# Two up-projections moved ahead of the output projection, and a biases' product moved behind the first down-projection

## The chip, the cores and the metric

The kernel runs on one core of one Trainium2 chip. The metric is the device time of one execution in microseconds (us), the median of several runs. The engines of the core are TensorE (PE, with its weight loads as PEld), VectorE (DVE), ScalarE (ACT), GpSimd (POOL) and SyncE (SP, which here only issues transfers).

## The reference

One transformer layer with modulation over x of 8 x 1024 x 256 (rows, tokens, channels), all in float32:

```
mod = silu(c) @ wmod                      # sa, ca, ga, sb, cb, gb per row; |ga|, |gb| >= 0.25
h = layernorm(x) * (1 + ca) + sa
x = x + ga * attention(h)
h = layernorm(x) * (1 + cb) + sb
x = x + gb * ffn(h)
```

The attention is linear: q and k of 16 heads (16 channels each) are scaled and clipped, Chebyshev polynomials are taken of both, of which the orders 1 to 5 have a weight, running sums over the tokens of T(k) v and of T(k) are built, and the output is the weighted sum of T(q) times the first, over the sum of T(q) times the second, followed by the output projection W_out.

The FFN has a shared expert and eight routed ones of 128 hidden channels: `silu(h W1 + b1) W2 + b2` for each. Every token takes its two best of the eight, weighted with sqrt(softplus(logit)):

```
hdn = silu(einsum('nd,edh->enh', h, rW1) + rb1)       # up-projection
y = einsum('enh,ehd->end', hdn, rW2) + rb2            # down-projection, second biases
routed = einsum('ne,end->nd', combine, y)
```

## The kernel before

The 8192 tokens are worked in 16 chunks of 512 (`CT`), two to a row, and number(i, p) = 2 i + p is a chunk's number. The program is a pipeline over chunks. `step(i, p, st)` exists once for each engine and does, for the stage of chunk c: the attention of chunk c; the first norm's transposes and the QKV projections of chunk c + 1 (`nxt`); the second norm, the router and its combine weights for chunk c - 1 (`prev`); and the nine experts of chunk c - 2 (`exp`). The dictionary `st` says which of these parts a stage has: two stages at the start (`FIRST`) and four at the end (`LAST`) have only some, twelve have all. The order of the work on each engine is the order in which its step is written out; there is no planner. Engines wait for each other with semaphores that count up.

Matrix products with float32 precision are split into high and low parts: `split_product` (line 1264) makes six matmuls of 512 columns of one product (two halves of the channels, and high x high, high x low, low x high). The high parts are written by ScalarE (`highs`, line 756), the low parts by VectorE from the same PSUM banks (`lows`, line 909): n1H, n1L for the first norm, n2H, n2L for the second. TensorE's queue in a full stage, in this order:

- up-projections of experts 0 and 1 (line 1264, inputs n2H, n2L, w1H, w1L) into the two banks of `ring`;
- `second_biases` (line 1372): four matmuls that put combine weights times second biases into the accumulators `acc`, with start set;
- transposes of the first norm (line 1255) into `tr`, behind the residual, which has read the projection from there; then up 2, down 0, four QKV projections, up 3, down 1;
- transposes of the second norm (line 1255), experts, router, head sums (line 1317), experts, the denominators (line 1330), experts 5 to 8;
- `project_out` (line 1341): eight products of the divided attention with W_out into `tr`, which wait for VectorE's `divide` (line 1029);
- `combine_by_expert` (lines 1353 and 1355): transposes of the split combine weights of chunk c - 1.

A down-projection (line 1383) of a routed expert waits until VectorE has multiplied the hidden state with the spread combine weights (`weigh_hidden`, line 1110). ScalarE writes that hidden state (`hidden`, silu, line 813) from the ring bank into one of three `hid` slots. The ring banks are used in a fixed order of 15 uses per full stage (`RING`, `ring_of`), and each use waits until the one two before has been copied out.

VectorE's queue at the turn of a stage: `divide` (1029), `output` (line 1119, the experts' sum times the gate), the odd orders of the next keys (925, 927); then, in the next stage, `residual` (1037, projection plus x, in two halves), statistics (367), odd orders of the queries, a weighting (943), `lows` of the first norm (909), more weightings and running sums (962), `weigh_hidden` of experts 1 and 2, a running sum, `lows` of the second norm.

The combine weights go to all partitions by way of DRAM: ScalarE copies them out of PSUM (`combine_rows`, 828 and 829), SyncE writes them to `cf_rows` (588), waits, and spreads them into `cfw` (592, for experts 1 to 6) and later the last two (598). GpSimd adds the experts' output to the stored x by an accumulating DMA (706). The inverse denominators go through DRAM in the same way (576, 581).

Of the kernel before, what the change touches and what calls it, by code (L numbers as in the profile page):

```python
# [8 lines left out]
P = 128  # L9
# [76 lines left out]
def build(nc, x_d, w_in_d, w_out_d, rout_d, ebias_d, sw1_d, sb1_d, sw2_d, sb2_d,  # L86
# [8 lines left out]
    with ctx:  # L95
# [185 lines left out]
        def number(i, p):  # L281
            return CB * i + p
# [463 lines left out]
        def _(act):  # L746
# [83 lines left out]

            def step(i, p, st):
                use = ring_of(i, p, st)
                nxt, prev, exp = later(i, p, 1), later(i, p, -1), later(i, p, -2)
# [9 lines left out]

                silu(0)
                silu(1)
                if qkv:
# [28 lines left out]
                if p == 1 and (not isinstance(i, int) or i < B):  # L875
                    row_biases(i, use if ffn else None)
                if second:
                    combine_rows(*prev)
# [5 lines left out]
            for q in range(2):  # L884
                for which in range(3):
                    square(0, 0, q, which)
            for i, p, st in FIRST:
                if number(i, p) == 1:
                    act.wait_ge(late_biases, 2)
                step(i, p, st)  # L890
            with act.Fori(1, B - 1) as i:
                for p in range(CB):
                    step(i, p, ALL)
            for i, p, st in LAST:
                step(i, p, st)

# [344 lines left out]
        def _(pe):  # L1241
# [123 lines left out]
            def second_biases(i, p):  # L1365


                c = number(i, p)
                pe.wait_ge(cf_ready, 2 * c + 2)
                ge(pe, ffn_gated, 2 * c)  # L1370
                for t in range(NT):
                    mm(acc[t // 2][:, t % 2], cfR[:, t * P:(t + 1) * P], r2[:, :], start=(t % 2 == 0), stop=False,
                       skip_group_check=True)

            def expert_down(i, p, use, e):

                c = number(i, p)
                if e:
                    pe.wait_ge(hidw_ready, E * c + e)
                else:  # L1380
                    pe.wait_ge(ring_copied, use["e0"][0] + 1)
                for t in range(NT):
                    last = mm(acc[t // 2][:, t % 2], hid[:, e % NG, t * P:(t + 1) * P], w2[:, e], start=False,  # L1383
                              stop=(e == E), skip_group_check=True)
                last.then_inc(expert_done, 1)

            def step(i, p, st):
                use = ring_of(i, p, st)
                nxt, prev, exp = later(i, p, 1), later(i, p, -1), later(i, p, -2)
# [7 lines left out]

                if ffn:
                    expert_up(*exp, use, 0)
                    expert_up(*exp, use, 1)  # L1400
                    second_biases(*exp)
                if qkv:
                    transposes(0, *nxt)
                if isinstance(i, int) and number(i, p) == 0:
                    bias_products()
                expert(0)
                if qkv:
                    for half in HALVES[:4]:
                        project(*nxt, use, half)
# [21 lines left out]
                expert(7)  # L1431
                expert(8)
                if attn_:
                    project_out(i, p)
# [13 lines left out]
            for half in HALVES:  # L1448
                project(0, 0, CHUNK0, half)
            for i, p, st in FIRST:  # L1450
                step(i, p, st)
            pe.wait_ge(late_weights, 2)
            pe.wait_ge(in_w2, 32)
            pe.wait_ge(s_r2, 4)
            for p in range(CB):
                step(1, p, ALL)
            with pe.Fori(2, B - 1) as i:
                for p in range(CB):
                    step(i, p, ALL)
            for i, p, st in LAST:  # L1460
                step(i, p, st)

# [24 lines left out]
```

## Time and profile before

| | us |
|---|---|
| median of 3 runs | 990.74 (985.78 to 991.19) |
| profiled execution | 988.04 |
| its span, first to last instruction | 986.3 |
| PE busy | 863.2 (88%) |
| DVE busy | 832.3 (84%) |
| POOL busy | 461.1 (47%) |
| ACT busy | 440.8 (45%) |
| mean granted TensorE clock | 0.955 |

All times of single instructions come from the profiled execution. Busy times are those of instructions that compute; matmuls are pipelined and their ends are modelled, so the modelled end of a group can lie after the start of the next. An idle time is given in brackets with what ended it.

### The profile page before, as it was taken

To read this page: it belongs to the slowest core of one execution; us is meant where nothing else is said; L and a number is where in the kernel's file an instruction comes from. 1 tells how busy PE (TensorE), PEld (TensorE's weight loads), DVE (VectorE), ACT (ScalarE), POOL (GpSimd) and SP (SyncE) were. 2 spreads that over 40 slices of the span, in tenths; PEclk is the share of its full clock that TensorE was granted. 3 is DMA by queue.
4 is the path that set the end of the run, shared out by engine and by line. 5 is a ranking of instruction groups with operands and counts; after the bars stand their busy time and mean duration, and the time that the engine had idled before them with its cause. 6 is when DMAs were issued, how large, how long until landed. Compare 5 with 4: busy or idle time off the path is not lost. (4 is left out here: it accounts for less than half of the span.)

```text
span 986.3 us, 14280 instructions
## 1 busy us (share of the span) xinstructions
PE 863.2 (88%) x4377; PEld 641.4 (65%) x4377; DVE 832.3 (84%) x1319; ACT 440.8 (45%) x637; POOL 461.1 (47%) x631
## 2 busy tenths in 40 slices
PE   3862658999898999999999999899999999978995
PEld 3641426676666767676767676686767676747784
DVE  2478798999899999999999999999999999987421
ACT  4253425363545545353635455554535363431420
POOL 2013445273546547472747365554837175453210
PEclk9777778999999999999999999999999999999998
DMA  7104133344452546353543536353634243443431
GB/s 256 49 1 87 43 68 127 75 102 128 74 160 66 151 88 161 65 142 77 117 120 72 149 69 176 68 150 80 167 65 125 69 103 113 79 128 75 126 108 21
DMA packets 51948, 101.03 MB, mean 102 GB/s; under 512 B 5347, under 2 KB 34606, under 8 KB 49846
## 3 DMA queue, kind: packets, MB, share of 16 engines
q1 hardware_dynamic: 35106, 65.45, 20.4%
q0 software_dynamic: 15360, 33.56, 19.9%
q10 hardware_dynamic: 1428, 1.43, 0.5%
q8 instruction: 18, 0.29, 0.1%
q14 instruction: 36, 0.29, 0.1%
HBM read 57.68 MB, written 17.58 MB: 76 GB/s over the span
## 5 line engine op out<-in xcount | busy, mean ns | idle before, releaser
L1383 PE MATMUL acc<-w,hid 128*128 128x256 f32 x1152 | 272.6, 382 | 14.6 <-DVE hid L1110 14.6
L1383 PEld LDWEIGHTS acc<-w,hid 128*128 128x128 f32 x1152 | 215.1, 190 | 58.9 <-DVE hid L1110 27.0
L813 ACT ACTIVATE hid<-ring,b1row 128x512 f32<-128x512 f32 x144 | 98.5, 684 | 180.3 <-PE ring L1264 179.0
L657 POOL DMA_DIRECT2D feat<-feat x48 | 46.5, 968 | 273.8 <-DVE feat L987 132.3
L1110 DVE TENSOR_TENSOR hid<-hid,cfw 128x512 f32<-128x512 f32 x128 | 92.9, 728 | 43.6 <-DMA cfw<-cf_rows 28.1
L768 ACT ACTIVATE feat<-ring,bqkv 128x512 f32<-128x512 f32 x96 | 66.1, 689 | 116.6 <-PE ring L1264 116.6
L1341 PE MATMUL tr<-wo_g,feat 128*128 128x256 f32 x256 | 67.1, 421 | 47.1 <-DVE feat L1029 47.1
L1264 PE MATMUL ring<-n2H,w1H 128*128 128x512 f32 x288 | 102.5, 437 | 0.0
L962 DVE TENSOR_TENSOR_SCAN feat<-zero,carry,feat 128x512 f32<-128x512 f32 x80 | 99.2, 1289 | 0.0
L962 DVE TENSOR_TENSOR_SCAN feat<-zero,feat 128x512 f32<-128x512 f32 x80 | 94.5, 1230 | 0.0
L1341 PEld LDWEIGHTS tr<-wo_g,feat 128*128 128x128 f32 x256 | 52.7, 211 | 61.0 <-DVE feat L1029 45.0
L1264 PE MATMUL ring<-n2H,w1L 128*128 128x512 f32 x288 | 90.5, 395 | 0.0
L1264 PE MATMUL ring<-n2L,w1H 128*128 128x512 f32 x288 | 90.4, 395 | 0.0
L1317 PE MATMUL tr<-feat,const 128*32 128x512 f32 x640 | 90.0, 608 | 0.0
L1264 PE MATMUL ring<-n1H,winH 128*128 128x512 f32 x192 | 68.4, 438 | 16.2 <-issue 14.5
L338 POOL TENSOR_TENSOR ms<-stats 128x4 f32<-128x4 f32 x32 | 42.3, 1323 | 73.3 <-DVE stats L367 68.6
L788 ACT ACTIVATE feat<-feat,const 128x1024 f32<-128x1024 f32 x64 | 70.0, 1141 | 1.0
L645 POOL TENSOR_TENSOR feat<-feat 128x1024 f32<-128x1024 f32 x16 | 53.3, 3330 | 30.1 <-DVE feat L927 30.1
L1264 PE MATMUL ring<-n1L,winH 128*128 128x512 f32 x192 | 62.7, 408 | 0.0
L1264 PEld LDWEIGHTS ring<-n2L,w1H 128*128 128x128 f32 x288 | 54.4, 189 | 12.5
L1264 PE MATMUL ring<-n1H,winL 128*128 128x512 f32 x192 | 62.5, 407 | 0.0
L1264 PEld LDWEIGHTS ring<-n2H,w1L 128*128 128x128 f32 x288 | 54.2, 188 | 12.6
(152 smaller groups left out, 1550.8 us busy)
## 6 DMA issues: line engine op xcount, KB each, us to landing
feat<-feat POOLq DMA_DIRECT2D x48, 512.0 KB, 4.6
cfw<-cf_rows SPq DMA_DIRECT2D x16, 1280.0 KB, 7.7
xin<-in_L_attn_x SPq DMA_DIRECT2D x16, 512.0 KB, 9.5
feat<-inv_rows SPq DMA_DIRECT2D x32, 256.0 KB
out<-x SPq DMA_DIRECT2D x16, 512.0 KB, 8.6
cfw<-cf_rows SPq DMA_DIRECT2D x16, 512.0 KB, 3.6
out<-fin POOLq DMA_DIRECT2D x16, 512.0 KB, 6.1
cfw<-cf_rows SPq DMA_DIRECT2D x16, 256.0 KB, 4.7
```

What stands on the lines that cost most here:

```text
L338: nc.gpsimd.tensor_tensor(t(0), m0, m1, ALU.add).then_inc(mv_steps[n], 1)
L645: g.tensor_tensor(f(W + 4), f(KT5), f(V0), ALU.mult).then_inc(weighted5, 1)
L657: g.dma_start(f(into), f(of), accum_op=ALU.add).then_inc(added[n], 16)
L768: a.activation(feat[:, (K0 + p, Q0 + p, V0)[m // 2], m % 2], ring[bank][:, :], ACT.Identity, bias=col(bqkv[:, (2, 3, 0, 1, 4, 5)[m]], i)). ...
L788: a.activation(f((qa, qb)[which - 1]), f(s), ACT.Square, bias=cv["biases"][:, which - 1:which]).then_inc(squares, 1)
L813: a.activation(hid[:, e % NG], ring[bank][:, :], ACT.Silu, bias=b1row[:, e:e + 1]).then_inc(ring_copied, 1)
L962: last = v.tensor_tensor_scan(feat[:, W + n, h], zero[:, 0:1].to_broadcast([P, CT]), feat[:, W + n, h], carry[:, n, h:h + 1] if p else 0.0 ...
L1110: v.tensor_tensor(hid[:, e % NG], hid[:, e % NG], cfw[:, (e - 1) % NW], ALU.mult).then_inc(hidw_ready, 1)
L1264: last = mm(out, w, x, start=(n == 0), stop=(n == len(terms) - 1))
L1317: last = mm(tr[q][g_ * QS:(g_ + 1) * QS, :], cv["headsum"][:, (r // HPH) * QS:(r // HPH + 1) * QS], feat[:, srcs[n], h], start=(n < 4 and ...
L1341: last = mm(tr[t // 2][:, (t % 2) * D:(t % 2 + 1) * D], attn[:, k, t * P:(t + 1) * P], wo_g[:, k], start=(k == 0), stop=(k == KD - 1))
L1383: last = mm(acc[t // 2][:, t % 2], hid[:, e % NG, t * P:(t + 1) * P], w2[:, e], start=False, stop=(e == E), skip_group_check=True)
```

## The change

On TensorE, the up-projections of experts 0 and 1 of a stage are issued in the stage before it: behind the last down-projection (`expert(8)`) and ahead of `project_out`, or, in a stage without attention, ahead of `combine_by_expert`. For that `step` is also given the next stage's parts (`st_next`) and its uses of the ring (`use_next`). `second_biases` moves from the head of the stage to behind the first down-projection. That down-projection now starts the accumulation (`start=True` for the first half of each bank) and takes over the wait for the accumulators to be free (`ffn_gated`); the biases' product continues it. On ScalarE, silu 0 and 1 of a stage move likewise to the end of the stage before, behind `row_biases` and ahead of `combine_rows`. Two waits for weights at the start are placed anew. VectorE, GpSimd and SyncE keep their programs.

```diff
             # ScalarE
-            def step(i, p, st):
-                use = ring_of(i, p, st)
+            def step(i, p, st, st_next):
+                use, use_next = ring_of(i, p, st), ring_of(*later(i, p, 1), st_next)
...
-                silu(0)
-                silu(1)
                 if qkv:
                     highs(0, *nxt)
                 silu(2)
...
                 if p == 1 and (not isinstance(i, int) or i < B):
                     row_biases(i, use if ffn else None)
+                if st_next["ffn"]:
+                    hidden(*prev, use_next, 0)
+                    hidden(*prev, use_next, 1)
                 if second:
                     combine_rows(*prev)
             # TensorE
                 pe.wait_ge(cf_ready, 2 * c + 2)
-                ge(pe, ffn_gated, 2 * c)
                 for t in range(NT):
-                    mm(acc[t // 2][:, t % 2], cfR[:, t * P:(t + 1) * P], r2[:, :], start=(t % 2 == 0), stop=False,
+                    mm(acc[t // 2][:, t % 2], cfR[:, t * P:(t + 1) * P], r2[:, :], start=False, stop=False,
                        skip_group_check=True)
...
                     pe.wait_ge(ring_copied, use["e0"][0] + 1)
+                    ge(pe, ffn_gated, 2 * c)
                 for t in range(NT):
-                    last = mm(acc[t // 2][:, t % 2], hid[:, e % NG, t * P:(t + 1) * P], w2[:, e], start=False,
-                              stop=(e == E), skip_group_check=True)
+                    last = mm(acc[t // 2][:, t % 2], hid[:, e % NG, t * P:(t + 1) * P], w2[:, e],
+                              start=(e == 0 and t % 2 == 0), stop=(e == E), skip_group_check=True)
...
-                if ffn:
-                    expert_up(*exp, use, 0)
-                    expert_up(*exp, use, 1)
-                    second_biases(*exp)
                 if qkv:
                     transposes(0, *nxt)
                 if isinstance(i, int) and number(i, p) == 0:
                     bias_products()
                 expert(0)
+                if ffn:
+                    second_biases(*exp)
...
                 expert(8)
+                if st_next["ffn"]:
+                    if isinstance(i, int) and number(i, p) == 1:
+                        pe.wait_ge(late_weights, 2)
+                    expert_up(*prev, use_next, 0)
+                    expert_up(*prev, use_next, 1)
                 if attn_:
                     project_out(i, p)
```

## Rows read from the trace of the kernel before

**Rows 1.** The page: busy us, share of the span, instructions of an engine.
```profile
PE 863.2 (88%) x4377; PEld 641.4 (65%) x4377; DVE 832.3 (84%) x1319; ACT 440.8 (45%) x637; POOL 461.1 (47%) x631
```
**Rows 2.** Waits, whole span: who waited for whom, us in total, times, longest.
```profile
PE tr L1341 <- DVE feat L1029: 47.1, 16, 13.3
...
DVE n2L L909 <- ACT n2H L756: 15.0, 14, 3.4
```
**Rows 3.** Timeline of PE: output projections and one QKV product; start, us, [idle before].
```profile
152.68 5.78 PE L1341 MATMUL tr<-wo_g,feat 128*128 128x256 f32 x16 [13.26 <-DVE feat L1029]
...
166.14 0.80 PE L1264 MATMUL ring<-n1H,winH 128*128 128x512 f32 x2
...
208.25 3.72 PE L1341 MATMUL tr<-wo_g,feat 128*128 128x256 f32 x16 [0.95 <-DVE feat L1029]
...
262.18 5.41 PE L1341 MATMUL tr<-wo_g,feat 128*128 128x256 f32 x16 [1.95 <-DVE feat L1029]
...
853.43 3.72 PE L1341 MATMUL tr<-wo_g,feat 128*128 128x256 f32 x16 [1.99 <-DVE feat L1029]
...
906.59 5.41 PE L1341 MATMUL tr<-wo_g,feat 128*128 128x256 f32 x16 [3.11 <-DVE feat L1029]
```
**Rows 4.** Timeline of PE over the turn of one inner stage.
```profile
532.48 3.72 PE L1341 MATMUL tr<-wo_g,feat 128*128 128x256 f32 x16 [1.13 <-DVE feat L1029]
...
536.39 0.71 PE L1264 MATMUL ring<-n2H,w1H 128*128 128x512 f32 x2
...
539.35 0.74 PE L1372 MATMUL acc<-r,cfR 50*128 50x256 f32 x4
...
542.34 1.89 PE L1383 MATMUL acc<-w,hid 128*128 128x256 f32 x8
543.88 0.81 PE L1264 MATMUL ring<-n1H,winH 128*128 128x512 f32 x2
```
**Rows 5.** Timeline of DVE over the same turn.
```profile
528.62 0.69 DVE L1110 TENSOR_TENSOR hid<-hid,cfw 128x512 f32<-128x512 f32 x1
...
535.89 1.27 DVE L1037 TENSOR_TENSOR x<-tr,xin 128x512 f32<-128x512 f32 x2
...
541.80 1.40 DVE L909 SCALAR_TENSOR_TENSOR n1L<-tr,mods,n1H 128x512 fp32r<-128x512 f32 x2
...
550.09 1.15 DVE L1110 TENSOR_TENSOR hid<-hid,cfw 128x512 f32<-128x512 f32 x1 [1.66 <-DMA cfw<-cf_rows]
...
554.36 1.41 DVE L909 SCALAR_TENSOR_TENSOR n2L<-tr,mods,n2H 128x512 fp32r<-128x512 f32 x2 [0.76 <-ACT n2H L756]
```
**Rows 6.** Timeline of DVE behind the projection at 152.68.
```profile
158.50 0.69 DVE L1037 TENSOR_TENSOR x<-tr,xin 128x512 f32<-128x512 f32 x1 [1.31 <-PE tr L1341]
...
163.83 1.40 DVE L909 SCALAR_TENSOR_TENSOR n1L<-tr,mods,n1H 128x512 fp32r<-128x512 f32 x2
```
**Rows 7.** Timeline of POOL: issues of the output's accumulating DMA, inner stage and last.
```profile
535.74 1.35 POOL L706 DMA_DIRECT2D out<-fin  x1 [0.85 <-POOL split L690]
...
946.70 1.33 POOL L706 DMA_DIRECT2D out<-fin  x1 [2.90 <-DVE fin L1119]
```
**Rows 8.** Timeline of SP: issues of the combine weights' copy and of their spread.
```profile
537.37 0.29 SPq L588 DMA_DIRECT2D cf_rows<-cfT  x1
541.83 0.82 SPq L592 DMA_DIRECT2D cfw<-cf_rows  x2
```
**Rows 9.** The chain that ended last, 906 to 980: start, us, what.
```profile
945.85 1.43 DMA cf_rows<-cfT
...
947.71 8.66 DMA cfw<-cf_rows
```
**Rows 10.** Windows: stretch, us, busy of each engine, then PEclk, the granted clock.
```profile
260.00:266.00 6.00, 4.05 (x12) 3.11 (x11) 5.06 (x7) 0.99 (x2) 3.60 (x7) 0.73 0.02 1
851.00:857.00 6.00, 4.01 (x20) 3.15 (x19) 5.03 (x7) 1.04 (x1) 3.54 (x7) 1.00 0.01 3
```

More of the change, by code:

```diff
@@ L886, in _ @@
                     square(0, 0, q, which)
-            for i, p, st in FIRST:
+            for n, (i, p, st) in enumerate(FIRST):
                 if number(i, p) == 1:
                     act.wait_ge(late_biases, 2)
-                step(i, p, st)
+                step(i, p, st, FIRST[1][2] if n == 0 else ALL)
             with act.Fori(1, B - 1) as i:
                 for p in range(CB):
-                    step(i, p, ALL)
-            for i, p, st in LAST:
-                step(i, p, st)
+                    step(i, p, ALL, ALL)
+            for n, (i, p, st) in enumerate(LAST):
+                step(i, p, st, LAST[n + 1][2] if n + 1 < len(LAST) else some())
         @block.vector
@@ L1381, in expert_down, with step @@
                     pe.wait_ge(ring_copied, use["e0"][0] + 1)
+                    ge(pe, ffn_gated, 2 * c)
                 for t in range(NT):
-                    last = mm(acc[t // 2][:, t % 2], hid[:, e % NG, t * P:(t + 1) * P], w2[:, e], start=False,
-                              stop=(e == E), skip_group_check=True)
+                    last = mm(acc[t // 2][:, t % 2], hid[:, e % NG, t * P:(t + 1) * P], w2[:, e],
+                              start=(e == 0 and t % 2 == 0), stop=(e == E), skip_group_check=True)
                 last.then_inc(expert_done, 1)
-            def step(i, p, st):
-                use = ring_of(i, p, st)
+            def step(i, p, st, st_next):
+                use, use_next = ring_of(i, p, st), ring_of(*later(i, p, 1), st_next)
                 nxt, prev, exp = later(i, p, 1), later(i, p, -1), later(i, p, -2)
@@ L1449, in _, with stages @@
                 project(0, 0, CHUNK0, half)
-            for i, p, st in FIRST:
-                step(i, p, st)
-            pe.wait_ge(late_weights, 2)
+            def stages(steps, after):
+                for n, (i, p, st) in enumerate(steps):
+                    step(i, p, st, steps[n + 1][2] if n + 1 < len(steps) else after)
+            stages(FIRST, ALL)
+            pe.wait_ge(s_r2, 4)
             pe.wait_ge(in_w2, 32)
-            pe.wait_ge(s_r2, 4)
-            for p in range(CB):
-                step(1, p, ALL)
+            stages([(1, p, ALL) for p in range(CB)], ALL)
             with pe.Fori(2, B - 1) as i:
[L1458 to L1461, printed above, removed]
+                stages([(i, p, ALL) for p in range(CB)], ALL)
+            stages(LAST, some())
 _INS = ['L0_attn_x', 'L0_attn_W_in', 'L0_attn_W_out', 'L0_ffn_routing_W', 'L0_ffn_expert_bias', 'L0_ffn_sW1',
```

## Prediction, made before the changed kernel ran

> **What bounds the kernel now.** I read the page's busy shares first: TensorE 88%, VectorE 84% [rows 1]. Both are averages with start and end in them, so I went on to the waits. TensorE's one regular wait is the one the change aims at: it stands before the output projection until VectorE has divided (L1029), 47.1 us over 16 times [rows 2]. Four of the sixteen are special (13.02, 13.26, 1.95, 3.11; three of them in rows 3); the other twelve, 0.95 to 1.99, leave 15.8 us, 1.31 each. VectorE's regular wait is for the second norm's high parts, 15.0 us in 14 times [rows 2].
>
> Then I laid the timelines of both engines over one inner stage. A stage is 53.8 us, (853.43 - 208.25) / 12 [rows 3]. TensorE goes from the projection at 532.48 to the first QKV matmul at 543.88 without a gap [rows 4]. VectorE, too, has no gap from the division to the low parts that end at 543.20; its only waits are 1.66 before the second expert's weighting (a DMA) and 0.76 before the second low parts at 554.36 [rows 5], and from there it is busy until the next division. So a stage is a loop through both: division, projection on TensorE, QKV, second norm, second low parts, then VectorE alone. The reader should see that VectorE has nearly as little slack as TensorE: the QKV product could start 0.68 earlier (543.88 less 543.20), and no more, before it waited for VectorE.
>
> **The projection is moved back.** The two up-projections with what follows take 539.35 - 536.39 = 2.96 us [rows 4]. The gap before the projection is 1.13 by the profile, but a group's modelled end lies after the moment the next can start: 542.34 + 1.89 - 543.88 = 0.35 [rows 4]. So the up-projections find 1.13 + 0.35 = 1.48 us of room, and the projection starts 2.96 - 1.48 = 1.48 later, at 533.96. The last down-projection can't move forward to make room: its hidden state is weighted at 528.62 + 0.69 [rows 5].
>
> **What waits for it.** VectorE's residual takes the two halves of the projection. Where it waited for the second half, it started 158.50 - 152.68 = 5.82 after the projection's start, for a group of 5.78 [rows 3, 6]; for one of 3.72 that is 3.76. So the second half is there at 537.72. VectorE wanted it at 535.89 + 1.27 - 0.68 = 536.48 (0.68 is one of the two) [rows 5]: a new stall of 1.24 us, with all of VectorE's queue behind it: statistics, odd orders, a weighting, and the low parts, which now end at 544.44. TensorE is by then through its queue: transposes wait for the residual (about 538.4), and transposes, third up-projection, first down-projection and the moved biases' product take 543.88 - 539.35 = 4.53 together [rows 4]; it is at the QKV product at about 543.0 and waits there for 544.44. The product starts 0.56 later than before (544.44 less 543.88), with about 0.1 of handover 0.66.
>
> From there to the second low parts it is TensorE and ScalarE back to back (554.36 - 543.88 = 10.48), so these come 0.66 later; VectorE's own arrival (553.60, plus the stall of 1.24 less what the wait of 1.66 takes up) is earlier. Behind them VectorE has no wait up to the next division but, in some stages, the one for the spread inverse, which moves along with VectorE. The mean gap is 1.31 instead of 1.13, so a mean stage loses 0.66 - 0.18 = 0.48.
>
> **The combine weights are late too.** Their transposes follow the projection, so the copy to DRAM (537.37) is issued up to 1.48 later. If the spread weights land as much later, VectorE reaches the second low parts at 553.60 + 1.48 = 555.08, a loss of 0.72 in this stage. If they land as before, 0.66 stands. What decides is the output's accumulating DMA, issued at 535.74 by GpSimd, which doesn't move [rows 7]: the small copy (16 KB) takes 4.46 us to the next issue behind it [rows 8], against 1.43 at the end, where it goes ahead of it [rows 9]. A copy issued later has less of it to wait for, so I take most of this as hidden. The Trainium skill says the same as a rule (DMA: Bandwidth & Descriptors, "Issuing engines are not separate DMA queues"): transfers of all engines share 16 DMA engines and interleave. By the rule the copy's landing hardly moves; were the queues separate, it would move by the full 1.48. The trace bears the rule out by 4.46 against 1.43.
>
> Twelve ordinary stages: 0.46 to 0.69 each, 5.5 to 8.3; I take 0.5, **+6.0**.
>
> **Free edits.** The second biases' product only changes places with work between the same two waits. Silu 0 and 1 move ahead of the combine rows on ScalarE; their inputs are there at 533.96, its next input only after the projection at 537.9, so that costs nothing where a projection lies between. Without that cover it would be one silu's tail, about 0.3, at the end below.
>
> **The end.** The last boundary has no output projection and no gap: the up-projections go before the combine transposes, and the chain runs through these, the copy, the spread (8.66 us) and so to the end [rows 9]. So +2.96 +0.3. Besides, the copy was issued 0.85 ahead of the output's DMA (945.85 against 946.70 [rows 7, 9]) and would now be behind it, where it took 4.46: between 0 and 3.0 more, part of it given back since the spread then meets less traffic. Bounds 2.9 to 6; I take **+4**.
>
> **The three special boundaries.** At 152.68 the gap takes the up-projections whole; the QKV product at 166.14 then starts behind the low parts' end at 165.23 [rows 3, 6]: **-0.8**. At 262.18 and 906.59 the projection took 5.41 instead of 3.72 [rows 3], under a granted clock of 0.73 over the six us, so partly at the half rate (1.2 GHz); another stage with the same gap kept 1.00 [rows 10]. If the filled gap keeps the clock up, each gives back up to 1.7, if not nothing (at 262.18 the projection would start 0.66 later, 2.96 - 1.95 - 0.35, and at 906.59 on time): **-0.5** and **-1.2**.
>
> Sum: 6.0 + 4 - 0.8 - 0.5 - 1.2 = +7.5 us. The profiled execution took 988.04 (span 986.3), so it would be 995.5; the median of the runs is 990.74, 2.7 above, which gives **998 us**. The forecast's own range is +4.6 (5.5 + 2.9 less 0.8 and 1.5 twice) to +13.5 (8.3 + 6 less 0.8).
>
> **Rivals.**
> 1. *The gain is real* (faster). If VectorE's low parts weren't the limit, the QKV product would start 1.48 earlier in each stage; twelve of 1.66 (room 1.31 + 0.35) and both clock falls, 23.3 us, less 4 at the end: -19, 971. It would take a slack on VectorE of more than 2 us where rows 4 and 5 show 0.68; it decides only if the residual doesn't wait for the moved projection. 0.10.
> 2. *Absorbed.* The stall stays under 0.7 us (half a projection handed over earlier than 3.76, or up-projections quicker next to others), the QKV product doesn't move, and only the end and the start count: 4 - 2.5 = +1.5, 992. For it: the first half is already there in time, and slack and loss are within 1 us of each other. Against it: the wait at 158.50, which ended with the projection's last half and not before [rows 6]. 0.19.
> 3. *Everything late.* The weights land 1.48 later each time and the end costs 6: 8.3 + 6 - 0.8 = +13, 1004. Against it: rows 7 to 9. 0.12.
> 4. *The clock falls in the new gap.* TensorE now waits 0.5 at the transposes and 1.4 before the QKV product. A gap of 1.95 was once followed by a fall worth 1.69 [rows 3, 10]. If that happens in nine of the twelve stages, 9 x 1.69 = 15 come on top of +7.5: +22, 1013. Against it: the twelve gaps of 0.95 to 1.99 behind which the group took its 3.72, and the new ones are shorter. 0.06. The Trainium skill (TensorE: Matmul & The Clock Gate, "Why this matters for your kernels") asks for no idle gaps between bursts of matmuls to keep the clock. By it the change gains where it closes the gaps of 1.95 and 3.11 (the -1.7 each) and risks the fall of rival 4 where it opens two. The trace agrees only in part: 1.95 fell, 1.99 didn't.
>
> **Chances.** Forecast 0.53, rivals 0.10, 0.19, 0.12, 0.06. A difference of 0.5%, about 5 us, is what a measurement of this kernel tells from none. Faster by more: rival 1, 0.10. Within: rival 2 and the forecast's lowest part, 0.23. Slower: the rest, 0.67. The range from 988 to 1007 leaves out rivals 1 and 4 and little else; it reaches down to rival 2 and up past rival 3.
>
> **What would show it.** In the changed profile: TensorE's wait before the projection is nearly gone, and a wait for n1L (L909) of 1 to 1.5 stands before the QKV product in most stages; VectorE waits for the projection (L1037) about 1.1 in each stage; the wait for n2H at L909 shrinks only slightly or vanishes; projection start to QKV start falls from 11.4 to about 10.6, while projection to projection grows from 53.8 by half a us; copy to spread at L588/L592 takes 3 to 3.5 us instead of 4.5. It is wrong if VectorE doesn't wait at L1037, if stages don't grow, or if TensorE's clock differs in the middle of the run.

## The result: 13 us slower, in the direction forecast and nearly twice its size

The changed kernel takes 1003.06 us in the median of 4 runs (1002.09 to 1003.26), beside 989.84 for the kernel before in the same set: ratio 1.0132, 95% interval 1.0093 to 1.017. Its profiled execution took 1002.91 (span 1001.2), 14.9 more than the one before. The forecast was +7.5, with a range up to 1007.

Page of the changed kernel, busy shares. Most line numbers of VectorE and TensorE are higher by one in the kernel after (projection L1342, division L1030, residual L1038, low parts L910, up-projections L1265, down-projections L1384):

```profile
PE 867.9 (87%) x4377; PEld 643.1 (64%) x4377; DVE 846.2 (85%) x1319; ACT 440.1 (44%) x637; POOL 444.4 (44%) x631
```

The shares are those of [rows 1] within a point, but for GpSimd's (44% instead of 47%), and don't show where 14.9 us went. The waits say more (engine, line, releaser: us in total, times, longest):

```profile
DVE hid L1111 <- DMA cfw<-cf_rows: 25.7, 7, 11.6
DVE x L1038 <- PE tr L1342: 18.8, 18, 1.6
...
DVE n2L L910 <- ACT n2H L756: 7.7, 12, 3.4
```

The wait that was aimed at [rows 2] is gone but for the first two stages (12.56 and 8.71) and 0.26 at the last, and VectorE now waits for the projection 18.8 us in 18 pieces. The same turn of an inner stage as in [rows 4], PE of the changed kernel:

```profile
535.89 3.62 PE L1342 MATMUL tr<-wo_g,feat 128*128 128x256 f32 x16
...
540.41 1.09 PE L1256 MATMUL tr<-const,ntok 128*128 128x128 f32 x8 [0.46 <-DVE x L1038]
...
542.74 1.89 PE L1384 MATMUL acc<-w,hid 128*128 128x256 f32 x8
544.55 0.73 PE L1372 MATMUL acc<-r,cfR 50*128 50x256 f32 x4
546.62 0.73 PE L1265 MATMUL ring<-n1H,winH 128*128 128x512 f32 x2 [1.33 <-DVE n1L L910]
```

And DVE, as in [rows 5]:

```profile
533.07 1.34 DVE L1030 TENSOR_TENSOR feat<-feat 128x512 f32<-128x512 f32 x2 [0.27 <-DMA feat<-inv_rows]
...
538.07 0.69 DVE L1038 TENSOR_TENSOR x<-tr,xin 128x512 f32<-128x512 f32 x1 [0.19 <-issue]
539.66 0.69 DVE L1038 TENSOR_TENSOR x<-tr,xin 128x512 f32<-128x512 f32 x1 [0.90 <-PE tr L1342]
...
544.98 1.40 DVE L910 SCALAR_TENSOR_TENSOR n1L<-tr,mods,n1H 128x512 fp32r<-128x512 f32 x2
...
557.01 1.41 DVE L910 SCALAR_TENSOR_TENSOR n2L<-tr,mods,n2H 128x512 fp32r<-128x512 f32 x2 [0.30 <-ACT n2H L756]
```

The projection starts 2.82 behind the division (before 1.4 to 1.5) and without a gap; the residual's second half waits 0.90, the transposes 0.46, the QKV product 1.33 for the low parts. Projection to QKV product is 546.62 - 535.89 = 10.73 (before 11.40), and the second low parts come 23.94 behind the division (before about 23.4).

### The profile page after: what moved, and what is told of

Same layout as the page of the kernel before. It is cut to its first block and busy times, and to the rows that moved or that the text cites. A ratio compares the mean times of both kernels' runs of the same rounds, so it can differ in the third digit from the quotient of the medians.

```text
span 1001.2 us, 14280 instructions
## 1 busy us (share of the span) xinstructions
PE 867.9 (87%) x4377; PEld 643.1 (64%) x4377; DVE 846.2 (85%) x1319; ACT 440.1 (44%) x637; POOL 444.4 (44%) x631
## 3 DMA queue, kind: packets, MB, share of 16 engines
q10 hardware_dynamic: 1428, 1.43, 0.5%
## 5 line engine op out<-in xcount | busy, mean ns | idle before, releaser
L1384 PE MATMUL acc<-w,hid 128*128 128x256 f32 x1152 | 277.9, 386 | 29.7 <-DVE hid L1111 29.7
L1384 PEld LDWEIGHTS acc<-w,hid 128*128 128x128 f32 x1152 | 217.2, 192 | 76.5 <-DVE hid L1111 43.5
L1111 DVE TENSOR_TENSOR hid<-hid,cfw 128x512 f32<-128x512 f32 x128 | 88.8, 695 | 43.7 <-DMA cfw<-cf_rows 25.7
L963 DVE TENSOR_TENSOR_SCAN feat<-zero,carry,feat 128x512 f32<-128x512 f32 x80 | 107.7, 1396 | 0.0
L1265 PE MATMUL ring<-n2H,w1H 128*128 128x512 f32 x288 | 104.3, 443 | 0.0
L1265 PE MATMUL ring<-n1H,winH 128*128 128x512 f32 x192 | 67.2, 432 | 32.9 <-issue 17.8
L963 DVE TENSOR_TENSOR_SCAN feat<-zero,feat 128x512 f32<-128x512 f32 x80 | 92.3, 1201 | 0.0
L1265 PE MATMUL ring<-n2L,w1H 128*128 128x512 f32 x288 | 91.2, 398 | 0.0
L1265 PE MATMUL ring<-n2H,w1L 128*128 128x512 f32 x288 | 90.9, 397 | 0.0
L1342 PE MATMUL tr<-wo_g,feat 128*128 128x256 f32 x256 | 62.6, 401 | 21.5 <-DVE feat L1030 21.5
L338 POOL TENSOR_TENSOR ms<-stats 128x4 f32<-128x4 f32 x32 | 33.3, 1039 | 88.1 <-DVE stats L367 83.5
L1342 PEld LDWEIGHTS tr<-wo_g,feat 128*128 128x128 f32 x256 | 51.4, 202 | 31.0 <-DVE feat L1030 22.9
L645 POOL TENSOR_TENSOR feat<-feat 128x1024 f32<-128x1024 f32 x16 | 53.0, 3315 | 30.0 <-DVE feat L928 30.0
L1265 PEld LDWEIGHTS ring<-n1H,winH 128*128 128x128 f32 x192 | 36.7, 199 | 44.8 <-issue 35.7
L1265 PEld LDWEIGHTS ring<-n2H,w1L 128*128 128x128 f32 x288 | 54.8, 190 | 12.9
L1265 PEld LDWEIGHTS ring<-n2L,w1H 128*128 128x128 f32 x288 | 54.8, 190 | 12.7
L1265 PEld LDWEIGHTS ring<-n2H,w1H 128*128 128x128 f32 x288 | 50.0, 191 | 19.4 <-issue 11.7
```

The lines of the kernel that those rows point to most:

```text
L338: nc.gpsimd.tensor_tensor(t(0), m0, m1, ALU.add).then_inc(mv_steps[n], 1)
L645: g.tensor_tensor(f(W + 4), f(KT5), f(V0), ALU.mult).then_inc(weighted5, 1)
L963: last = v.tensor_tensor_scan(feat[:, W + n, h], zero[:, 0:1].to_broadcast([P, CT]), feat[:, W + n, h], carry[:, n, h:h + 1] if p else 0.0 ...
L1111: v.tensor_tensor(hid[:, e % NG], hid[:, e % NG], cfw[:, (e - 1) % NW], ALU.mult).then_inc(hidw_ready, 1)
L1265: last = mm(out, w, x, start=(n == 0), stop=(n == len(terms) - 1))
L1342: last = mm(tr[t // 2][:, (t % 2) * D:(t % 2 + 1) * D], attn[:, k, t * P:(t + 1) * P], wo_g[:, k], start=(k == 0), stop=(k == KD - 1))
```

## Where the 14.9 us are

I took the start of each division as the mark of a stage (numbered 0 to 15 here) and compared the two profiled executions.

| stretch | before | after | difference |
|---|---|---|---|
| start to division 0 | 96.62 | 95.63 | -1.0 |
| 0 to 2 | 110.23 | 110.52 | +0.3 |
| 2 to 3 | 53.94 | 53.60 | -0.3 |
| 3 to 4 | 55.96 | 55.12 | -0.8 |
| 4 to 14, ten stages | 535.22 | 544.94 | +9.7 |
| 14 to 15 | 53.27 | 52.36 | -0.9 |
| 15 to the end of the span | 81.06 | 89.03 | +8.0 |

The ten stages split once more, at the second low parts: +5.1 from division to these (0.51 a stage in the mean, 0.1 to 0.8 in each), +4.65 from these to the next division. The latter lies in the odd stages. Four of the five took 29.7 to 30.2 there and now take 31.2 to 31.5; the fifth, stage 9, had taken 31.3 before and takes 31.1. The even stages are 0.1 shorter in the mean.

One execution of each kernel is little for such small differences. The kernel with the biases alone and the one with only the last boundary changed (both below) leave the ups of these ten stages where they were: 539.6 and 536.3 beside the 535.2 of before, mean 537.0. The up-projections alone and the last boundary as before leave them moved: 546.5 and 544.0 beside 544.9, mean 545.1. So the ten stages lose about 8, and the two parts are +3.2 (0.32 a stage) and +4.8 in the mean of three executions each.

One of the odd stages in the kernel before, first the timeline of DVE, then that of POOL:

```profile
501.00 1.41 DVE L909 SCALAR_TENSOR_TENSOR n2L<-tr,mods,n2H 128x512 fp32r<-128x512 f32 x2 [0.72 <-ACT n2H L756]
502.33 1.21 DVE L987 SCALAR_TENSOR_TENSOR feat<-feat 128x1024 f32<-128x1024 f32 x1
503.46 1.22 DVE L983 TENSOR_TENSOR feat<-feat 128x1024 f32<-128x1024 f32 x1
```
```profile
500.71 1.30 POOL L713 TENSOR_TENSOR wo_g<-wo,gates 128x512 f32<-128x512 f32 x1 [0.45 <-DMA gates<-gate_rows]
```

The same stage of the changed kernel:

```profile
495.06 3.43 DVE L946 SCALAR_TENSOR_TENSOR feat<-feat 128x1024 f32<-128x1024 f32 x1
498.41 0.68 DVE L1111 TENSOR_TENSOR hid<-hid,cfw 128x512 f32<-128x512 f32 x1
...
503.13 1.22 DVE L988 SCALAR_TENSOR_TENSOR feat<-feat 128x1024 f32<-128x1024 f32 x1
504.26 2.32 DVE L984 TENSOR_TENSOR feat<-feat 128x1024 f32<-128x1024 f32 x1
```
```profile
494.50 2.90 POOL L645 TENSOR_TENSOR feat<-feat 128x1024 f32<-128x1024 f32 x1
503.15 2.35 POOL L713 TENSOR_TENSOR wo_g<-wo,gates 128x512 f32<-128x512 f32 x1 [5.75 <-DMA gates<-gate_rows]
```

Once per row of the batch, in the odd stages, GpSimd scales W_out by the gates (L713). Before, that took 1.30 us and began about where VectorE waits for the second high parts (22.9 to 23.9 behind the division in four rows of six), so that it ran beside the low parts, which took their 1.41 all the same; in the changed kernel it comes at 25.2 to 26.0 in all six. Here it starts at 503.15, under VectorE's order products, and each holds up the other: L713 takes 2.35, and L984, begun at 504.26, ends 1.08 behind it at 506.58 and takes 2.32 instead of 1.22. In stage 9 the product before it (L988) is the stretched one (2.27), in stage 13 the weighting of a hidden state behind it (L1111, 1.78); in stage 9 of the kernel before it was L987 (2.32). L713 comes later here because VectorE, late by the stall, now starts its weighting L946 (495.06) just behind GpSimd's L645 (494.50): 3.43 instead of 1.22. The weighting of the next hidden state is late by that, and SP's load of the gates waits in its queue behind the weights' issue that this releases. SP of before, then of after:

```profile
495.88 0.33 SPq L598 DMA_DIRECT2D cfw<-cf_rows  x1
496.25 0.91 SPq L569 DMA_DIRECT2D gates<-gate_rows  x2
```
```profile
499.11 0.33 SPq L598 DMA_DIRECT2D cfw<-cf_rows  x1
499.49 0.91 SPq L569 DMA_DIRECT2D gates<-gate_rows  x2
```

The Trainium skill has the rule (SBUF — State Buffer, "Who interferes with whom"): a VectorE instruction with two SBUF inputs and a GpSimd instruction that reads SBUF shut each other out for a whole instruction, and the one begun first wins. These rows agree: L984 ends 1.08 behind L713, and L946 1.09 behind L645's end at 497.40.

All traces together bear it out. In the eleven traces of kernels that scale all of W_out (the experiments below among them) there are 55 such odd stages, five in each. In 27 of them L713 starts 24.4 or more behind the division, and from the second low parts to the next division they take 31.0 to 32.0. In the other 28 it starts at 23.9 or before, and they take 29.2 to 30.5. The changed kernel has five of the first kind in five, the kernel before one in five.

The end, in the chain of the changed kernel (start, us, what), against [rows 9]:

```profile
926.93 3.15 PE acc L1384 x8
930.08 1.40 PE tr L1256 x8
...
957.02 3.83 DMA cf_rows<-cfT
960.92 4.81 DMA cfw<-cf_rows
966.57 3.78 PE acc L1384 x8
970.36 2.20 PE ring L1265 x6
972.55 1.73 PE acc L1384 x8
```

The copy of the combine weights (957.02) takes 3.83 now, and the output's DMA was issued 2.2 ahead of it (954.81; for before [rows 7, 9]). Two groups on the chain, at 926.93 and 966.57, take 3.15 and 3.78 where the group takes 1.7 to 2.0 else. TensorE had stood idle before both, and the windows show its clock (the stretch, its length, busy of PE, PEld, DVE, ACT and POOL, PEclk, DMA share, GB/s):

```profile
926.90:930.90 4.00, 3.97 (x13) 3.28 (x14) 0.69 (x1) 0.00 (x0) 0.00 (x0) 0.59 0.67 251
966.50:970.50 4.00, 3.93 (x9) 3.20 (x10) 1.31 (x3) 0.00 (x0) 0.00 (x0) 0.50 0.16 69
```
```profile
926.93 3.15 PE L1384 MATMUL acc<-w,hid 128*128 128x256 f32 x8 [3.90 <-DVE hid L1111]
...
966.57 3.78 PE L1384 MATMUL acc<-w,hid 128*128 128x256 f32 x8 [5.12 <-DVE hid L1111]
```

A granted clock of 0.50 is the lower level, 1.2 GHz; at the same places of the kernel before it was 1.00.

From division 15 to the third down-projection of the last stage (972.39 after, 957.21 before) is 60.22 against 51.97, +8.25:

- the up-projections and a silu ahead of the last combine transposes: 2.76 + 0.28 = +3.0
- the boundary before it: +1.2 by the time of the copy's issue (D + 44.85 against D + 40.61, less the 3.0)
- the copy behind the output's DMA +2.4, but TensorE now waits for the first of the two transfers of the spread, not the second, -4.2: together -1.8
- from those weights to the third down-projection of the stage 6.61 instead of 0.79, +5.8: one more expert stands behind them (3.2), and half clock stretches it (3.78 + 2.20 on the chain instead of 1.99 + 1.40, 2.6).

Another 0.28 comes back behind that.

## Experiments

Each was timed in five rounds beside the kernel before, which took 989.26, 990.49 and 987.70 in the median in the three sets. Diffs are against the changed kernel, but for the first and for the smaller scaling on the kernel before.

**The biases alone** (on the kernel before).

```
 stage head:
-                    second_biases(*exp)          # behind expert_up(..., 1)
...
                 expert(0)
+                if ffn:
+                    second_biases(*exp)
...                                               # start= of the group moves to down-projection 0
```

> Only the second biases' product is moved behind the first down-projection; both up-projections stay at the head of the stage. My theory (the loss comes from the projection issued late behind the up-projections) expects no change: TensorE's queue from the projection to the QKV product is as long as before (11.4 us), 988 to 991. A theory in which the down-projection that now starts the accumulation, or the wait for the accumulators moved with it, costs something expects part of the 13 us here.

990.26 us, ratio 1.0005 (0.9977 to 1.0032): no cost by itself that this can tell. Its profiled execution spent 53.96 in each of the ten stages, 0.44 more than the one of the kernel before, with medians 1 apart. So much do two executions of like kernels differ; two of its five odd stages have the late scaling.

**The up-projections alone.** The same edit undone on the changed kernel; ups and silus stay ahead.

> Only the up-projections and their silus are moved ahead; the second biases' product stays at the head of the stage and starts the accumulation. My theory expects the whole loss here: 1002 to 1004, with the same stall of about 0.9 us before the second half of the residual and a QKV product that waits for n1L. The wait of 0.46 us at the first norm's transposes should be filled by the biases' product in part. If the loss needs both edits, the time is nearer to 990.

999.95 us, ratio 1.0114 (1.0083 to 1.0145): most of the loss, though 2 below the expected range. Its profiled execution was the slowest of the five. Its ten inner stages take 54.64 each, as the changed kernel's 54.49. Its end took 84.8 from division 15, and shows what the changed kernel's 89.0 is made of. Chain of this kernel:

```profile
931.38 1.99 PE acc L1384 x8
...
959.79 3.95 DMA cf_rows<-cfT
963.80 4.47 DMA cfw<-cf_rows
...
969.11 1.99 PE acc L1384 x8
971.11 1.39 PE ring L1265 x6
```

The copy is as slow (3.95), the order is the same, and TensorE waited before 969.11 too (3.23), but the clock held. So the end costs 84.84 - 81.06 = +3.8 without the two falls, and the falls carry most of the other 4.

**One up-projection ahead.**

```
                     hidden(*prev, use_next, 0)
-                    hidden(*prev, use_next, 1)
...
                     expert_up(*prev, use_next, 0)
-                    expert_up(*prev, use_next, 1)
...                                               # both back to their places of before
```

> The changed kernel, but only up-projection 0 (and silu 0) is issued ahead; up-projection 1 stays at the head of the next stage. One takes 1.48 us, about what there is of room before the projection (1.31 + 0.35). My theory: the projection is on time, VectorE doesn't stall at the residual, and the QKV product can start up to 0.6 earlier than before the change, bounded by n1L: 0.3 to 0.6 in each of 11 stages gained, 1.2 to 3 lost at the end: 984 to 990. If the loss were proportional to what is moved (by any cause that counts instructions and not room) it would be half of 13: 996.

988.49 us, ratio 0.9992 (0.9965 to 1.0019). The residual doesn't wait; the QKV product starts 12.28 behind the division instead of 12.9 and waits 0.65 for the low parts: of the room of 0.68 read from rows 4 it won 0.6, and the low parts hold it there. A stage keeps 0.24 of that: the ten take 53.28 each (before 53.52).

**The last boundary as before.**

```
-                if st_next["ffn"]:
+                if st_next["ffn"] and not (isinstance(i, int) and i == B):
...                                               # ups 0, 1 and silus 0, 1 of that stage at its head
```

> The changed kernel, but at the last boundary (stage 16 to 17, without an output projection) both up-projections and their silus stay at the head of the last stage, as before the change. From the trace of the changed kernel the part from the last division to the end is 89.0 us against 81.1 before. My theory: 2.8 of it is the up-projections in front of the combine transposes, 2.4 the copy of the weights that now falls behind the output's accumulating DMA, 2.7 a TensorE that has waited 5.1 us and restarts at the half rate, 1.2 the same at the boundary before. So the tail is back to about 82.3 and the time is 995.5 to 997.5. If the end is late for what happened earlier, nothing changes: 1003.

996.55 us, ratio 1.0067 (1.0041 to 1.0093). The stretch behind division 15 is 82.2 instead of 89.0. It still has the clock fall at the boundary before the last (group of 3.55 behind a wait of 3.96, at 927.76). SP and POOL of this kernel: the copy goes first again and takes 1.49 to the next issue:

```profile
954.65 0.28 SPq L588 DMA_DIRECT2D cf_rows<-cfT  x1
956.14 0.79 SPq L592 DMA_DIRECT2D cfw<-cf_rows  x2
```
```profile
955.50 1.33 POOL L706 DMA_DIRECT2D out<-fin  x1 [2.89 <-DVE fin L1123]
```

**The up-projections behind the projection**, ahead of the combine transposes.

```
+                if attn_:
+                    project_out(i, p)
                 if st_next["ffn"]:
...
-                if attn_:
-                    project_out(i, p)
```

> The changed kernel, but with both up-projections between the output projection and the combine transposes: the projection is on time, the combine weights are 2.96 us late (more than the 1.2 of the changed kernel). Theory of the late projection: no stall at the residual, the QKV product starts 11.4 after the projection as before; what is left is the end (about +7) and some wait for the late weights, 995 to 1001. Theory of the late combine weights: the loss per stage is larger than in the changed kernel, 1010 or more.

1001.75 us, ratio 1.0145 (1.0109 to 1.018), 0.75 outside the first range. VectorE of this kernel:

```profile
537.87 1.34 DVE L1030 TENSOR_TENSOR feat<-feat 128x512 f32<-128x512 f32 x2
...
542.75 1.28 DVE L1038 TENSOR_TENSOR x<-tr,xin 128x512 f32<-128x512 f32 x2
...
548.67 1.40 DVE L910 SCALAR_TENSOR_TENSOR n1L<-tr,mods,n1H 128x512 fp32r<-128x512 f32 x2
```

The residual has both halves at once, the QKV product starts 12.99 behind the division, and the second low parts 23.1 to 23.5: the loss ahead of these is gone. The weights came only a little later: their copy starts 9.3 behind the division (6.3 before), their spread at 10.7 to 11.5 (9.3 to 11.0 before). The rest, +0.41 per stage, is the stretched L984 (2.32) in all five odd stages. But L946 isn't stretched in this kernel. VectorE of stage 7 (division at 483.44):

```profile
499.69 1.22 DVE L946 SCALAR_TENSOR_TENSOR feat<-feat 128x1024 f32<-128x1024 f32 x1
...
502.23 1.94 DVE L1111 TENSOR_TENSOR hid<-hid,cfw 128x512 f32<-128x512 f32 x1 [1.32 <-DMA cfw<-cf_rows]
```

Here the weighting of the hidden state is late because it waits for the spread weights and then takes 1.94; SP issues the gates at 504.57, 21.1 behind the division, and the scaling starts at 25.0. So the stretched L946 is one way to a late scaling, and late weights are another; what they share is the late weighting that SP waits for.

The total is no better than the changed kernel's, since this execution had two early clock falls (projections of 5.41 in stages 2 and 3; +5.2 by division 4) and an end of 89.7.

**A smaller scaling of W_out, on the changed kernel and on the kernel before.** From the second row on GpSimd scales one column of W_out only, so the rest of the projection's weights keep the first row's gates; left out is all but one column of that product.

```
+                if isinstance(i, int) and i == 0:
                     g.tensor_tensor(wo_g[:, :, :], wo[:, :, :], ga, ALU.mult).then_inc(wo_ready, 1)
+                else:
+                    g.tensor_tensor(wo_g[:, :, 0:1], wo[:, :, 0:1], gates[:, 0:1, 0:1]...
```

> The changed kernel, with GpSimd's scaling of W_out by the row's gate cut to one column for all rows but the first (left out: the scaling of the other 255 columns; the output of rows 1 to 7 is projected with the first row's gate). In the changed kernel's trace this instruction (1.3 to 2.4 us) falls beside a product of VectorE (2.3 instead of 1.2 us) in six stages of seven. If the two engines shut each other out there, six times 1.1 us go: 996 to 998. If VectorE's product is slow for another reason (its own operands, a DMA), the time stays at 1003.

> The kernel before, with the same cut of the W_out scaling (the output of rows 1 to 7 is projected with the first row's gate). There the scaling fell into VectorE's own wait before the second low parts in four stages of six and beside a product in two or three. If that is why the change lost more than the late projection explains, the cut gives only 2 to 3 us here, 986 to 988, less than half of what it gives on the changed kernel.

On the kernel before 987.59, ratio 0.9973 (0.9945 to 1.0), 2.9 less than the kernel before in its set. On the changed one 1001.17, ratio 1.0108 (1.0072 to 1.0144), which is 2 us less than the change and not 6, and the intervals overlap. The time on the kernel before is the expected one, but the cut gave no more on the changed kernel than there, against both expectations. The stage times say something else. The stretched L984 is gone from all stages, and the odd ones take 29.7 to 30.3 behind the second low parts (31.1 to 31.5 in the changed kernel), also where the small scaling starts as late as 25.9. But four stages (4, 7, 9, 12) lost the gain ahead of them. TensorE of this kernel in one, and the window:

```profile
323.64 0.73 PE L1375 MATMUL acc<-r,cfR 50*128 50x256 f32 x4
325.71 0.72 PE L1268 MATMUL ring<-n1H,winH 128*128 128x512 f32 x2 [1.34 <-DVE n1L L913]
326.28 1.01 PE L1268 MATMUL ring<-n1L,winH 128*128 128x512 f32 x2
327.09 1.05 PE L1268 MATMUL ring<-n1H,winL 128*128 128x512 f32 x2
```
```profile
326.00:330.00 4.00, 4.00 (x12) 3.09 (x12) 4.00 (x5) 0.69 (x1) 3.92 (x4) 0.57 0.93 337
```

Behind the new gap of 1.34 before the QKV product the clock fell, and the second low parts came at 25.3 to 25.6 instead of 24.0 (24.5 in stage 7, whose projection had come early). The window's clock was 0.57 or 0.58 in all four. In the changed kernel the same gap stands in nearly every inner stage, and the clock kept 1.00 in the three windows taken (from 328, 382 and 437). The ten stages took 545.0 in this execution, as the changed kernel's 544.9: what the smaller scaling gave, the clock took. So the stretched product is what the scaling does to the stage; the total doesn't prove its price.

**One up-projection ahead, at all boundaries but the last**, the edits of the third and fourth together.

> One up-projection (and silu 0) issued ahead at all boundaries but the last, the biases' product behind the first down-projection. The same with the last boundary included took 988.5; its stages are 0.24 us shorter than before the change and its end is 1.1 longer. I expect the 1.1 to 2 us of the end back: 986.5 to 987.5, 2 to 3 us below the kernel before, about what five rounds can just tell. A theory in which any work moved ahead of the projection costs expects 989 or more.

982.61 us, ratio 0.9917 (0.9887 to 0.9947), faster than the kernel before by 0.8%, more than expected. It was run again beside the one-up kernel, since their first profiles had nearly the same end (82.6 and 82.2) and so didn't seem to say what set them apart.

> One up-projection ahead at all boundaries but the last, again. If the version really beats both kernels: 0.990 to 0.995 of before. If its first result was helped by scatter: 0.996 to 0.999, and the same as the kernel with one ahead everywhere.

> The same kernel as in the run with one up-projection ahead at every boundary, beside the kernel with one ahead at all but the last. In the profiles both had the same last stretch (82.2 and 82.6 us), so what set them apart in the medians (988.5 against 982.6) is not placed. If the last boundary costs what it seems to, this one is again 0.5 to 0.8% slower than the other, 0.999 of the kernel before; if the difference was scatter between the two sets of runs, the two come out within 0.3% of each other, both at 0.994 to 0.997 of before.

Again 982.88, ratio 0.9946 (0.9916 to 0.9976), against 986.34, ratio 0.9976 (0.995 to 1.0001), for one up everywhere. Both sets have it faster than before. Against the one-up kernel it is 0.35% faster, between the two expectations, and the intervals overlap. Its first profile is 5.8 below the one before: 3.7 between divisions 0 and 4 (the fall at 262 is avoided), 1.7 in the ten stages (53.35), 1.75 ahead of division 0, which is scatter, and -1.6 behind division 15. The one-up kernel's second profile had an end of 85.6: its group at 916.03 took 3.78 where the first run's at 914.77 took 1.99. The same instructions meet the fall in one execution and not in another.

What the last boundary costs with one up can be read once the falls are set apart. The end of 82.2 (one up everywhere) had none, the end of 82.6 (all but the last) had one at the boundary before:

```profile
912.67 3.68 PE L1386 MATMUL acc<-w,hid 128*128 128x256 f32 x8 [2.54 <-DVE hid L1113]
```

From this group to the next down-projection on the chain it is 5.94, against 4.26 without a fall, so the fall cost 1.7. Without it the last copy would have gone out about 40.2 behind division 15 instead of 41.84; with one up at the last boundary it went out at 41.55. That is 1.4, the time of one up-projection, and from the copy to the end of the span both take 40.6 to 40.8. The rest of the 3.5 between the medians is not placed.

**Only the last boundary** changed (the rest as in the kernel before, with the biases moved).

```
-                if st_next["ffn"]:
+                if st_next["ffn"] and isinstance(i, int) and i == B:
...                                               # all other stages begin as before
```

> Kernel before with the second biases behind the first down-projection, and the two up-projections and silus ahead only at the very last boundary, where no output projection lies between. If the end term of the changed kernel is the last boundary's own (its combine transposes 2.8 later, the small copy behind the output's DMA, one more expert behind the weights, and TensorE's slower clock behind the wait), this costs 6 to 7 us against the kernel before: ratio 1.006 to 1.007, and from the last division to the end of the span 87 to 88 us instead of 81. If it costs only the 2.8 to 3 of the up-projections themselves, 1.003 and 84. If the end term needs the other boundaries as well, 1.000 and 81 to 82.

993.36 us, ratio 1.0059 (1.0029 to 1.0088), and 86.3 from division 15 to the end: +5.3. The copy again takes 3.81, the wait before the second down-projection 4.64, and that group 3.19. It misses its range by a little. The kernel that put this boundary back had gained 6.8 by its end; 0.9 of the 1.5 between the two is the fall, which cost 2.6 there and 1.7 here (959.26 to 964.30, against 3.38 without one).

## Why the prediction was right, and what it mis-sized

The direction and the first link were right. The size was not: of the 14.9 us between the profiles the sum had 7.5. The time fell within the range because the range had been drawn past the third rival, whose number (1004) is nearly the measured one, while its mechanism, weights that land 1.48 later each time, did not happen. That part is luck.

**The late projection: right.** Forecast: second half 3.76 behind the projection's start (measured 3.77), QKV product held by the low parts, 0.66 later (0.68 in the stage shown), 0.5 a stage. Measured 0.51 in this pair of executions and 0.32 in the mean of three executions each, so the agreement to the hundredth is chance. With the residual unstalled (ups behind the projection) the loss vanished; with half the work ahead it turned into a small gain.

**The combine weights: right in outcome, not in the reason.** The copy went out about 1.2 later, and its spread followed after 2.4 (540.68 to 543.07) instead of 4.46 [rows 8] or the 3 to 3.5 forecast, so the spread came earlier than before and the weighting didn't wait. The forecast held GpSimd's issue still; in this stage it went out 3.37 behind the division instead of 4.73. The Trainium skill's rule cited in the forecast fits the end as well: the copy took 3.83 where it was issued 2.2 behind the output's DMA and 1.43 where it went ahead. It doesn't say when the copy lands; the last section has that from the traces.

**A term put at nothing: +4.65 in ten stages.** I followed VectorE's stall to the low parts and wrote that behind them VectorE has no wait, so that the stage loses the delay and no more. I did not ask what GpSimd does while VectorE is late. Its scaling of W_out had run in and beside a wait of VectorE's, and now starts under its products. That a late scaling costs the stage 1.2 us in the mean (31.3 against 30.05 behind the second low parts) is shown by the 55 stages, and that it goes with the scaling by the kernels with the small one. How the scaling comes to be late is read from the traces: the weighting that releases SP's queue is late, here by the stretched L946, with the ups behind the projection by late weights. No run moved the scaling by itself.

**The end: the mis-sized term.** Forecast +4 and, for a clock fall not had at 906.59, -1.2: +2.8. Measured +8.0. The +4 was good: the last boundary alone cost 5.3 with a fall of 1.7 in it. The -1.2 failed. The kernel with the last boundary as before has that term by itself, and its end costs +1.1, a fall included; in the up-projections' run, without a fall, the last copy's issue (43.43 less the 3.0 of the ups, against 40.61) gained 0.2. The projection did take 3.72 instead of 5.41, and the copy of the combine weights was issued 1.69 earlier behind the division. But it was now 3.05 behind the output's DMA instead of 4.74, and took 3.38 to the next issue instead of 1.84. The weights were there only 0.5 earlier (14.02 behind the division, before 14.52). With two up-projections fewer ahead of them, TensorE stood 3.90 and met a fall there; another followed at 966.57. This is the forecast's fourth rival at a place where it hadn't been expected; in its own place, before the QKV product, it did not appear in the three windows of the changed kernel, but did in four stages of the kernel with the small scaling.

**The three special boundaries.** At 262.18 the fall was avoided (-0.84, forecast -0.5). Behind 152.68 the gain came as forecast: the QKV product starts 14.19 behind the division instead of 15.00, the second low parts 0.9 earlier. It was lost again behind them, where L984 takes 2.32 beside a scaling of 1.71; the two stages together come to +0.3. Stages 2 and 14 came out 0.3 and 0.9 shorter, not longer, and why is open.

Against the sum of 7.5: ordinary stages 6.0, measured 9.7 - 0.9 - 0.3 = 8.5; start -1.3, measured 0.3 - 0.8 = -0.5; end 2.8, measured 8.0; and -1.0 of scatter ahead of division 0. That makes 14.9 with the unrounded figures. (The forecast's lower bound of +4.6 took 1.5 for each clock fall where the working had up to 1.7; with that it is +4.2, and nothing else changes.)

## To carry to other kernels

Where two engines pass work to each other in a loop, read the room of both before filling a gap of one. Here TensorE had 1.48 us and VectorE 0.68: 2.96 us of work in the gap made VectorE wait 1.1 for the projection, and half of it won 0.6 at the QKV product and 0.24 a stage. When a change delays VectorE, lay GpSimd's SBUF work beside the new times and not only the queue behind the stall. Work taken out ahead of a transfer that lands with another one wins little and comes back as idle time of TensorE, and the group behind it may run at half clock.

## What the runs showed of the hardware that I hadn't expected

- VectorE's 128x1024 products of 1.22 us take 2.32 when GpSimd's L713 stands between two of them (1.30 else, up to 2.38 there), and 3.43 just behind the start of GpSimd's L645 (2.90).
- TensorE's clock doesn't follow the length of a gap alone: it fell behind idle times of 1.34 us (0.57), 3.90 (0.59) and 5.12 (0.50), and held behind 1.33 in the same place of the changed kernel and behind 3.23 at the end of the kernel with the up-projections alone. The one-up kernel had a group of 1.99 (behind 2.30) in one execution and of 3.78 (behind 3.10) in another.
- The 16 KB copy of the combine weights, issued 1.2 to 4.5 behind GpSimd's accumulating DMA, is done about when that is (6.0 from issue to landing in the changed kernel), and not a fixed time behind its own issue. In all thirteen traces there are 195 copies with such a DMA near. From copy to spread, by the distance of the copy's issue behind the DMA's: ahead by 0.85 or behind by 0.8, 1.5 us (8 copies); behind by 1.2 to 2, 2.9 to 5.3 (26); by 2.2 to 3.2, 3.0 to 4.2 (104); by 3.2 to 4, 2.3 to 3.2 (11); by 4 to 4.5, 1.7 to 2.6 (25); by 4.5 to 5, 1.5 to 2.1 (10); by more, 1.5 (11). From 2.2 to 4.5 the spread follows 6.0 to 7.2 behind the output's issue, whenever the copy was issued. So the order of issue alone doesn't decide: the one-up kernel issued the copy 0.8 behind at the last boundary (941.77 against 940.96) and it took 1.47.
